# Attention probabilities turned by VectorE block transposes and a trip through DRAM, with their low plane made on GpSimd

## The reference

```
q = norm(x[b]) @ Wq[g]            # 128 x 4*128
k, v = ctx[b] @ Wk[g], ctx[b] @ Wv[g]
q, k = rope(q, k)                 # layer 0;  rmsnorm(q), rmsnorm(k) in layers 1 and 3
p = softmax(q @ k.T / sqrt(128) + mask)
x[b] += tanh(gate) * (p @ v) @ Wo[g]
```

## Time and profile before

| | |
|---|---|
| runs | 2681.81 us median of 3 (2679.26 to 2682.94) |
| profiled execution, span | 2680.3 us |
| TensorE busy | 2458.8 us, 92% |
| VectorE, ScalarE, GpSimd busy | 1818.8, 1264.2 and 1241.2 us |
| chain that ended last | TensorE 73%, VectorE 7%, DMA 6%, GpSimd 5%, issue 5%, ScalarE 3% |
| DMA | 191.67 MB, mean 72 GB/s |

### The profile page before, as it was taken

How to read it: one execution, slowest core, us unless ns; L and a number is a source line. 1 busy time by engine, 2 the same in 40 slices (tenths; PEclk the granted TensorE clock), 3 DMA queues, 4 the chain that set the end, 5 groups by cost and what they waited for, 6 DMA issues and landing times.

```text
span 2680.3 us, 42144 instructions
## 1 busy us (share of the span) xinstructions
PE 2458.8 (92%) x13741; PEld 2088.5 (78%) x13741; DVE 1818.8 (68%) x3407; ACT 1264.2 (47%) x3698; POOL 1241.2 (46%) x1382
## 2 busy tenths in 40 slices
PE   5899999998889999999987888899689999999977
PEld 4788888887778888888776776676578888888853
DVE  4677777767777777777665776563477777777762
ACT  2455555554246555555533545223245555555520
POOL 4645545554235444444434666423444444444443
PEclk9999999999999999999999999899899999999979
DMA  3112222331112111111100000159501111100154
GB/s 107 63 52 99 84 96 84 103 103 56 48 56 95 40 40 33 34 34 37 60 28 17 1 1 26 67 192 358 177 28 49 34 36 40 40 32 25 41 198 147
DMA packets 67884, 191.67 MB, mean 72 GB/s; under 512 B 10097, under 2 KB 10737, under 8 KB 64730
## 3 DMA queue, kind: packets, MB, share of 16 engines
q1 hardware_dynamic: 51936, 139.85, 15.4%
q0 software_dynamic: 10224, 42.03, 4.5%
q10 hardware_dynamic: 5514, 7.11, 0.8%
HBM read 170.57 MB, written 52.14 MB: 83 GB/s over the span
## 4 chain that ended last, share of the span: by engine, by line
PE 73%; DVE 7%; DMA 6%; POOL 5%; issue 5%; ACT 3%; ACTq 0%; SPq 0%; POOLq 0%; DVEq 0%
PE B_qkv L761 30%; PE B_out L761 19%; PE B_more L837 4%; PE B_s L817 4%; DMA slots_y<-S 3%; PE B_qT L807 3%; PE B_more L827 3%; PE B_s L818 2%; PE B_more L761 1%; DMA out_x<-rows_last 1%; DVE X L1578 1%; PE B_more L911 1%; DVE xn L1461 1%; DMA raw<-in_pieces 1%; PE B_out L809 1%
## 5 line engine op out<-in xcount | busy, mean ns | idle before, releaser
L1283 ACT ACTIVATE W<-S,nmx 128x128 f32<-128x128 f32 x768 | 297.6, 394 | 49.7 <-DVE nmx L1560 49.6
L2085 POOL TENSOR_SCALAR rn<-ss 128x5 f32<-128x5 f32 x128 | 25.5, 199 | 609.7 <-DVE ss L1503 609.7
L1180 ACT ACTIVATE sq<-B_qkv 128x640 f32<-128x640 f32 x127 | 89.6, 706 | 409.1 <-PE B_qkv L761 409.1
L2106 POOL TENSOR_TENSOR S<-S,mask 128x512 f32<-128x512 f32 x192 | 251.4, 1310 | 16.5 <-ACT S L1116 16.3
L1578 DVE SCALAR_TENSOR_TENSOR X<-B_out,gates,X 128x512 f32<-128x512 f32 x200 | 150.3, 751 | 151.7 <-PE B_out L761 151.7
L2145 POOL TENSOR_TENSOR W<-W,rden 128x512 f32<-128x512 f32 x192 | 199.9, 1041 | 88.6 <-DVE rden L1565 88.3
L761 PE MATMUL B_qkv<-ring_h,xnT_h 128*128 128x512 f32 x540 | 215.8, 400 | 9.8 <-DVE spare_l L1412 4.0
L761 PE MATMUL B_out<-ring_h,oT_h 128*128 128x512 f32 x516 | 206.0, 399 | 14.5 <-DVE kT L1550 9.1
L817 PE MATMUL B_s<-kT,qT_h 128*128 128x256 f32 x768 | 204.6, 343 | 12.1 <-DVE xnT_l L1412 9.9
L761 PE MATMUL B_qkv<-ring_l,xnT_h 128*128 128x512 f32 x540 | 214.3, 397 | 0.0
L761 PE MATMUL B_qkv<-ring_h,xnT_l 128*128 128x512 f32 x540 | 212.4, 393 | 0.0
(11 more groups left out here) (504 smaller groups left out, 7923.5 us busy)
## 6 DMA issues: line engine op xcount, KB each, us to landing
raw<-in_pieces SPq DMA_DIRECT2D x270, 256.0 KB
slots_x<-in_zero SPq DMA_DIRECT2D x32, 1030.0 KB, 6.7
raw<-in_experts SPq DMA_DIRECT2D x16, 768.0 KB, 7.2
w<-in_experts SPq DMA_DIRECT2D x8, 1024.0 KB, 16.8
slots_y<-S SPq DMA_DIRECT2D x31, 256.0 KB
xn<-slots_x ACTq DMA_DIRECT2D x8, 257.5 KB, 6.3
raw<-in_ctxT SPq DMA_DIRECT2D x8, 256.0 KB
X<-in_x ACTq DMA_DIRECT2D x8, 256.0 KB, 2.6
```

The source lines that it names most:

```text
L1283: t = act.activation(W[:, k, cols(r)], S[:, k, cols(r)], ACT.Exp, bias=nmx[:, k, r:r + 1], accum_out=den[:, k, r:r + 1])
L2106: pool.tensor_tensor(S3, S3, m.unsqueeze(1).to_broadcast([P, R, P]), ALU.add).then_inc(*masked.now((layer, u)))
```

## The change

`turn_p` is gone. Its work is done in four steps for each unit:

- `blocks_p` (i+3, 31), VectorE: after GpSimd has normalised W, one transpose instruction turns each block of 32 x 32 within W and writes to S, in an order by blocks.
- `store_p` (i+3, 32), SP: S goes to a DRAM tensor of 256 KB (one for each k), rows of 2 KB.
- `load_p` (i+3, 62), SP: after the store has landed, the tensor comes back to W in runs of 512 bytes, so that the blocks are across partitions where they belong.
- `split_p` (i+4, 30): ScalarE copies W to pT_h, now from SBUF and in another order; GpSimd subtracts, for pT_l, in place of VectorE.

The keys come out in an order that is permuted by 32 and 4. So the masks are permuted on the host, and the copies of kT read and write with strides. exp waits for GpSimd's split_p before it writes W again, and the low scores wait for the store before they write S again.

```diff
-            self.at(i + lag - 2, 46 if first_turn else 30, "turn_p", layer, u)
+            self.at(i + 3, 31, "blocks_p", layer, u)
+            self.at(i + 3, 32, "store_p", layer, u)
+            self.at(i + 3, 62, "load_p", layer, u)
+            self.at(i + lag - 2, 46 if first_turn else 30, "split_p", layer, u)
...
+        between_p = [nc.dram_tensor(f"between_p{k}", (P * HG,), F32).ap() for k in range(2)]
...
+        def blocks_first(ap):
+            return ap.rearrange("p (j h q) -> p h j q", j=BLOCKS, q=BLOCK)
+        def by_block(ap):
+            return ap.rearrange("p (i r q) -> p r i q", i=BLOCKS, q=BLOCK)
+        def heads_first(ap):
+            return ap.rearrange("p (r i q) -> p r i q", i=BLOCKS, q=BLOCK)
+        def turned_keys(ap):
+            return ap.rearrange("p (a j) -> p j a", j=BLOCKS)
+        def block_keys(ap):
+            return ap.rearrange("p (j a) -> p j a", j=BLOCKS)
...
-            def turn_p(layer, u):                         # TensorE
-                k = unit(layer, u)[3]
-                pe.wait_ge(*probs.of((layer, u)))
-                bank_free("pt")
-                for r in range(R):
-                    t = pe.transpose(B_pt[:, cols(r)], W[:, k, cols(r)], ident[:, :])
...
             def times_v(layer, u):
-                pe.wait_ge(*pT_lo.of((layer, u)))
+                pe.wait_ge(*p_split.of((layer, u)))
...
-                copy(kT[0], B_out[:, 0:P], scale).then_inc(*kT_hi.now((layer, u)))
+                copy(block_keys(kT[0]), turned_keys(B_out[:, 0:P]), scale).then_inc(*kT_hi.now((layer, u)))
...
+                elif k in S_reader:                       # low_scores, ScalarE
+                    act.wait_ge(*S_reader[k])
...
-                W_reader[k] = [p_turned.of((layer, u))]
+                W_reader[k] = [p_split.of((layer, u))]
+                S_reader[k] = p_stored[k].of((layer, u))
...
+            def split_p(layer, u):                        # ScalarE
+                k = unit(layer, u)[3]
+                act.wait_ge(*p_loaded[k].of((layer, u)))
                 for sem, value in pT_reader:
                     act.wait_ge(sem, value)
-                copy(pT[0][:, :], B_pt[:, :]).then_inc(*pT_hi.now((layer, u)))
+                copy(heads_first(pT[0][:, :]), by_block(W[:, k, :])).then_inc(*pT_hi.now((layer, u)))
...
-            def turn_p(layer, u):                         # VectorE
-                dve.wait_ge(*pT_hi.of((layer, u)))
-                sub(pT[1][:, :], B_pt[:, :], f32(pT[0][:, :])).then_inc(*pT_lo.now((layer, u)))
+            def blocks_p(layer, u):
+                k = unit(layer, u)[3]
+                dve.wait_ge(*probs.of((layer, u)))
+                dve.transpose(blocks_first(S[:, k, :]), W[:, k, :].rearrange("p (r j q) -> p r j q", r=R, q=BLOCK)
+                              ).then_inc(*blocks_made.now((layer, u)))
...
+            def split_p(layer, u):                        # GpSimd
+                k = unit(layer, u)[3]
+                pool.wait_ge(*pT_hi.of((layer, u)))
+                pool.tensor_tensor(heads_first(pT[1][:, :]), by_block(W[:, k, :]), heads_first(f32(pT[0][:, :])), ALU.subtract
+                                   ).then_inc(*p_split.now((layer, u)))
...
+            def store_p(layer, u):                        # SP
+                k = unit(layer, u)[3]
+                sync.wait_ge(*blocks_made.of((layer, u)))
+                if p_loaded[k].made:
+                    sync.wait_ge(p_loaded[k].sem, p_loaded[k].by * p_loaded[k].made)
+                sync.dma_start(between_p[k].rearrange("(p n) -> p n", p=P), S[:, k, :]).then_inc(*p_stored[k].now((layer, u)))
+            def load_p(layer, u):
+                k = unit(layer, u)[3]
+                sync.wait_ge(*p_stored[k].of((layer, u)))
+                sync.dma_start(W[:, k, :].rearrange("p (i n) -> p i n", i=BLOCKS),
+                               between_p[k].rearrange("(i p n) -> p i n", i=BLOCKS, p=P)).then_inc(*p_loaded[k].now((layer, u)))
...
-        "mask13": i["mask_1x1xSxS2_ff0"].reshape(P, P),
+        "mask13": _keys_by_block(i["mask_1x1xSxS2_ff0"].reshape(P, P)),
```

35 lines of the change are left out of this document (20 added, 15 removed).

## The result

The changed kernel takes 2724.3 us (median; 2720.7 to 2727.9), the kernel before 2681.6: a ratio of 1.0155, 95% interval 1.0137 to 1.0172, or +42.7 us. The forecast was 2699. The sign was right, and the time lies in the wide range of 2660 to 2760, but not in the forecast's own of 2687 to 2717: the loss is two and a half times the +17 that I had worked out. The profiled execution, by its own time of 2720.7 us, is the fastest of the four.

The account below looks back on a forecast made before the run. TensorE was taken to bound three full stretches at 9.49 us a unit. Terms -13.7 + 13.7 + 2 + 3 + 1 + 11 = +17 us on the 2680.3 span, forecast 2699 us; range 2660 to 2760, its own 2687 to 2717.

Parts of the forecast that it names:

- Heads and tails: Outside the full stretches: four early units +3, drains of layers 0 and 1 +1, end of layer 3 +11 us.
- Layers 1 and 3: TensorE gains only 0.13 us in each of 105 units before waiting for qk: -13.7 us in all.
- Layer 0: GpSimd's subtraction meets weight splits and delays the mask, S and v_l: +13.7 us; clears ahead of load_p: about +2.
- with a weight split they wait for GpSimd anyway ... up to about 1.2 us it costs nothing: VectorE's block transpose, with split, qT_l, kT_l and S queued behind it, was claimed free up to about 1.2 us.
- Rival 1: TensorE's gain survives in layer 0, GpSimd's subtraction not delaying v_l: 2665 us with the tail, 2654 without; chance 0.15.
- Start, heads and drains: Four units before 125.98 us bound by the GpSimd cycle, +3; drains of layers 0 and 1, +1.
- The end: End of layer 3: store_p of unit 62 queues behind the experts' eight 1 MB loads, delaying times_v: +11 us.
- The trip: Store and load through DRAM take 5.2 to 9.6 us, taken as 5.4, with 7.0 us free.
- Rival 3: The trip is late in every unit: from 7.9 us each microsecond counts on 153 units; 2791 at 8.5; chance 0.14.
- Rivals 2 and 4: Respectively: tail hidden, layers 0 and 1 cancel, 2688 us, chance 0.14; full 0.36 us gained everywhere, 2640, chance 0.05.

Follow-up runs that it names:

- e1: Changed kernel with the experts' eight loads issued after the last load_p: 2718.2 us, ratio 1.0143.
- e7: Kernel before, with one of TensorE's four transposes of P per unit after the first and nothing added: 2654.0 us, ratio 0.9892.
- e5: Changed kernel with the 32 clears issued in layer 2 instead of layer 0: 2718.6 us, ratio 1.0128.
- e9: Changed kernel without the trip through DRAM and with GpSimd's subtraction cut to 16 columns: 2664.4 us, ratio 0.9939.
- e13: e9 with the block transpose issued behind qT_l and kT on VectorE: 2654.6 us, ratio 0.9908.
- e15: Changed kernel with split_p issued behind the mask instead of in front of it: 2702.4 us, ratio 1.0090.
- e3: Changed kernel with GpSimd's new subtraction cut from 512 to 16 columns after the first unit: 2695.3 us, ratio 1.0053.
- e8: Kernel before, with the change made only in units 4 to 51 of layers 1 and 3: 2675.9 us, ratio 0.9981.
- e10: Kernel before, with only kT copied in the new order of keys by strided copies: 2681.5 us, ratio 0.9995.
- e11: e8 once more, over more rounds: 2675.5 us, ratio 0.9986.
- e2: Changed kernel without store_p and load_p, ScalarE waiting for the block transpose: 2701.5 us, ratio 1.0077.
- e6: Changed kernel with subtraction cut to 16 columns, clears in layer 2 and experts' loads behind the last load_p: 2676.2 us, ratio 0.9981.
- e14: Changed kernel with block transpose and store behind qT_l and kT: 2790.0 us, ratio 1.0410.
- e16: Changed kernel with block transpose behind qT_l and kT, split_p behind the mask, experts' loads behind the last load_p: 2774.1 us, ratio 1.0345.

## Why the prediction was off, point by point

The step that failed is "Heads and tails". It priced the longer way of a unit at +3 for four units and +1 for the drains, nothing for the start, and at the end the queue of the experts' loads alone (+11). Measured are +16.0 before the end, 11.2 of it from the start to unit 67, and +17.6 at the end, where 7.4 stay with the queue's part out (e1). The terms of the full stretches came out within 3 us in this profile, in layer 0 by errors that cancel.

- **Layers 1 and 3: right.** Forecast 9.36 us a unit and a wait of 0.2 for qk; measured 9.36 to 9.37 and 0.26. The terms are -5.0 and -5.7 in place of -6.4 and -7.3: 0.12 a unit, less single units of 9.6 to 10.2. e7 shows the limit alone.
- **Layer 0: the mechanism right, the sum right by luck.** Forecast +13.7 for GpSimd and +2 for the clears, measured +15.7. GpSimd's part was put too high: without clears the 48 units come to +8.7 (e5), kind by kind within 0.2 us of the forecast. The clears were put too low: +6.4 in this profile, which is of the fastest execution, and +13.4 against the second one; I had looked at load_p's lateness in some 5 units alone. Opened up further by e5, e9 and e13: GpSimd's subtraction +14.3 (9.3 to -5.0), VectorE's place in front +12.3 (-5.0 to -17.3), against -17.3 that TensorE gives; each figure holds with the causes named before it out, and another order would share them otherwise. Of the step "with a weight split they wait for GpSimd anyway ... up to about 1.2 us it costs nothing" the first half held in the unit shown, but only by 0.27 us: with the subtraction cut, the same place costs 12.3 us.
- **Rival 1: refuted** in the kernel after (layer 0 takes 9.80 us a unit on average), but by queue order and not by GpSimd's load: in e15 GpSimd does as much, behind the mask, and layer 0 is at -3.0. Part of that gain can be the trip's, as e15 wants the loaded W later too (waits of 19.1 us for it against 33.8); the 10 units with GpSimd's split alone, at 9.08 in place of 9.69, owe theirs to the order.
- **Start, heads and drains: the first large miss.** Forecast +4 in all, measured 16.0 (4.5, 2.1, 4.6, 3.3, 1.5), of which the 3.3 and the 1.5 are no more than unchanged stretches show. I had priced the cycle there and the trip's length. Shown: 2.4 of the start is VectorE's place (e13), the 2.1 after it and some 6.7 from unit 57 to 67 are GpSimd's subtraction (e3). Some 1.5 of the start is left unexplained, or 2.5 to 2.8 against the starts of e8, e10 and e11.
- **The end: the mechanism right, the size off.** Forecast +11, measured +17.6. The queue's part is 10.2 (e1) and was well put. Missed were the 7.4 and 7.5 us that remain without the queue's part (e1) or without any trip (e2). With the subtraction cut as well 3.5 are left beside the trip (e6) and -0.1 without it (e9): each unit of the drain has a longer serial path, which nothing covers there. Between the units 58 and 61 one sees it at work: +5.0 us in the kernel after, +1.2 with the subtraction cut (e3). I took the cover of the full stretches for granted in the empty ones.
- **The trip: right in the full stretches**, 2.0 + 3.0 where I had 5.4. ScalarE waits 33.8 us for it in layer 0, with the clears, 4.9 in layer 1's stretch and nothing in layer 3's. Rival 3 is refuted for this kernel, but its threshold was near: e14, with the store 1.5 us later and behind the clears, shows the price in layer 0.
- **Rivals 2 and 4: refuted.** The end is not hidden, and the units of layers 1 and 3 take 9.36 or 9.37 us (median), not 9.13. (The forecast's sum is 2697.3 us of span, not the 2697.4 written there.)

The 21.5 us that the sum lacked are +4.5 before the first unit, -0.9 in the units after it, +4.1 and +1.5 in the heads and drains at units 57 to 67 and 128 to 132, +2.8 in the stretch of layer 2, +3.0 in the steady units, +6.6 at the end: for the most part where the working was shortest. The medians differ by 42.7 us and not by 38.5, as the profiled execution of after is 3.6 us under its median.

## What to carry to other kernels

Work taken from the full engine pays only up to the next chain, and here that chain could be read in advance to 0.01 us from one unit; but the operations that replace it lengthen every serial path, and starts, drains and ends have no cover for them, so walk these with the same care as the full stretches. An operation that waits belongs in its engine's queue behind everything that does not need it, and a transfer that something waits for belongs in a queue without bulk loads ahead of it; after every move, recount what now stands in front of it on each queue, the DMA queue included. When the whole scatters by more than the effect, read marks inside the span instead, and compare the profiled execution's own time with the median of its runs before trusting a single profile. A term that comes out right can be two errors that cancel: open it by kinds of unit before calling it right.

## What the runs showed that was not expected

- A block transpose of 128x512 in 32x32 blocks on VectorE takes 0.71 us in SBUF, as much as the reduction of that shape.
- The mask on GpSimd went from 1310 to 1495 ns on average, with its work unchanged. The traces say why: a mask that begins while a weight split runs on VectorE takes 1.60 us in layer 0 and 1.74 in layers 1 and 3 (means of 35 and 67), the others 1.18 and 1.31. Before, 24 of the 192 masks began so, after it is 102, as the subtraction in front delays them; with the subtraction cut to 16 columns (e9) it is 2, and the mean is 1255 ns. The rule that the prediction drew from the Trainium skill (SBUF — State Buffer, Who interferes with whom) fits that, also the other way round: a split on VectorE that begins while GpSimd's subtraction runs takes 1.13 us (median), one that meets nothing 0.68.
- A 256 KB store behind eight loads of 1 MB landed after 15.1 us, one behind a single 1030 KB clear after 7.8 (run e16), the median of all 192 after 2.0.
- Copies of 128x128 with a stride of four elements took ScalarE and VectorE no longer than plain ones (371 against 370 ns on ScalarE, 334 against 336 on VectorE, medians of 128).
